# A mixture-of-experts stage as one block, with each tile's results added to the tokens' rows in DRAM

## The reference

```
logits = xf @ router_w + router_b                      # 8 experts
topk_vals, topk_idx = lax.top_k(logits, 2)
gates  = softmax over the two chosen, 0 elsewhere
routed = silu(xf @ w1[e]) * (xf @ w3[e]) @ w2[e]        # for each expert e
y      = sum_e gates[:, e] * routed[e], and two shared experts; both halves weighted 0.5
```

## Time and profile before

| | us |
|---|---|
| median of three runs | 3865.52 (3856.92 to 3866.49) |
| the profiled execution's own time | 3864.73 |
| its span | 3862.7 |

### The profile page before, as it was taken

The page is one execution under the profiler, slowest core; times in us unless marked ns, Lnnn a source line. Parts: engine busy times, 40 slices in busy tenths (PEclk is TensorE's granted clock), DMA queues, the critical chain, the costliest instruction groups (busy, mean ns, idle before and its releaser), DMA issues. The chain is left out here.

```text
span 3862.7 us, 72003 instructions
## 1 busy us (share of the span) xinstructions
PE 3120.2 (81%) x24192; PEld 2382.7 (62%) x24192; DVE 2530.4 (66%) x5327; ACT 1824.5 (47%) x3241; POOL 1631.9 (42%) x1347
## 2 busy tenths in 40 slices
PE   5999688888799889688507999999999996995880
PEld 4888577777688778576404555555555554884660
DVE  5666577877566678555375777777777765774552
ACT  2444244444355445255303666666666664543550
POOL 1665222222366545456552333333333332553665
PEclk9999899999899989799857999999999997987995
DMA  3000000000000022355443324324233221224547
GB/s 110 0 0 0 16 0 0 0 0 0 1 0 0 19 77 74 105 161 158 149 143 101 93 70 114 82 78 111 74 88 100 74 66 64 77 74 156 158 151 281
DMA packets 204552, 292.07 MB, mean 76 GB/s; under 512 B 21472, under 2 KB 136560, under 8 KB 204416
## 3 DMA queue, kind: packets, MB, share of 16 engines
q1 hardware_dynamic: 149760, 189.51, 17.8%
q0 software_dynamic: 27264, 75.01, 5.1%
q10 hardware_dynamic: 27392, 25.83, 2.0%
HBM read 146.47 MB, written 143.28 MB: 75 GB/s over the span
## 5 line engine op out<-in xcount | busy, mean ns | idle before, releaser
L1945 DVE TENSOR_REDUCE neg_max_sb<-s_ps 128x1 f32<-128x512 f32 x1024 | 692.4, 687 | 292.4 <-PE s_ps L1672 271.6
L1835 ACT ACTIVATE prob_sb<-s_ps 128x512 f32<-128x512 f32 x1024 | 602.5, 600 | 393.6 <-PE s_ps L1684 384.3
L1592 POOL TENSOR_TENSOR prob_sb<-prob_sb,band_sb 128x520 f32<-128x520 f32 (+1 forms) x256 | 285.2, 1114 | 715.5 <-ACT prob_sb L1835 715.3
L529 POOL TENSOR_TENSOR f_sq_lo_sb<-f_sq_sb,f_sq_hi_sb 128x512 fp32r<-128x512 f32 x256 | 329.5, 1295 | 348.4 <-ACT f_sq_hi_sb L504 348.4
L1684 PE MATMUL s_ps<-q_stack_sb,k_stack_sb 128*128 128x512 f32 x1024 | 450.9, 441 | 8.0 <-ACT prob_sb L1835 7.5
L1672 PE MATMUL s_ps<-k_stack_sb,q_stack_sb 96*128 96x512 f32 x1024 | 425.9, 419 | 33.6 <-DMA k_stack_sb<-qk_scratch 23.3
L1280 POOL DMA_INDIRECT ranked_rows<-m_y_gated_sb,slot_dest_sb x312 | 328.0, 1051 | 263.5 <-ACT m_y_gated_sb L1261 177.5
L946 POOL DMA_INDIRECT expert_rows<-rows_sb,row_index_sb x256 | 258.0, 1008 | 245.3 <-DVE row_index_sb L1045 173.6
L1684 PEld LDWEIGHTS s_ps<-q_stack_sb,k_stack_sb 128*128 128x128 f32 x1024 | 193.2, 189 | 256.7 <-ACT prob_sb L1835 131.3
L499 ACT ACTIVATE f_relu_sb<-ffn_hp_ps 128x512 f32<-128x512 f32 x256 | 153.4, 599 | 314.6 <-PE ffn_hp_ps L452 314.0
L1705 PE MATMUL pv_ps<-prob_sb,v_ones_sb 128*32 128x512 f32 x2048 | 273.2, 606 | 0.9 <-POOL prob_sb L1592 0.9
(11 more groups left out here) (346 smaller groups left out, 7936.9 us busy)
## 6 DMA issues: line engine op xcount, KB each, us to landing
expert_in_sb<-expert_rows SPq DMA_DIRECT2D x78, 520.0 KB
qk_scratch<-qk_hi_sb SPq DMA_DIRECT2D x128, 256.0 KB
q_stack_sb<-qk_scratch SPq DMA_DIRECT2D x128, 192.0 KB, 4.0
k_stack_sb<-qk_scratch SPq DMA_DIRECT2D x128, 192.0 KB, 4.2
token_results_sb<-ranked_rows SPq DMA_DIRECT2D x32, 512.0 KB, 6.3
token_results_sb<-ranked_rows ACTq DMA_DIRECT2D x32, 512.0 KB, 6.0
qk_scratch<-qk_lo_sb SPq DMA_DIRECT2D x64, 256.0 KB
expert_rows<-zero_rows_sb ACTq DMA_DIRECT2D x16, 520.0 KB, 5.6
```

The costliest lines, as they stand in the source:

```text
L529: nc.gpsimd.tensor_tensor(sql[:, j, :], sq[:, j % 2, :], as_f32(sqh[:, j, :]), ALU.subtract).then_inc(low_ready, 1)
L1592: nc.gpsimd.tensor_tensor(pr, pr, bcast(band[:, off:off + hi - lo].unsqueeze(1), [P, GH, hi - lo]), ALU.mult).then_inc(band_done, 1)
L1835: nc.scalar.activation(prob[:, kt % 2, i, :], s2p[i % 2][:, :], ACT.Exp).then_inc(exp_done, 1)
L1945: nc.vector.tensor_reduce(nm[:, g % 2, 2 * (i % 2) + i // 2, qt:qt + 1], s1p[n % 2][:, :], AXIS_X, ALU.max, negate=True).then_inc(max_done, 1)
```

## The change

It consists of five parts.

1. **GLA.** ACT takes over `norm.normalise` and `o_norm`, as `activation(Identity, bias=-mean*rstd, scale=rstd)`; DVE only makes the factors. SP writes zeros over all of `expert_rows` (70144 rows of 1040 bytes) in four DMAs beside the stage, which ends only when they have landed.
2. **MoE weights.** `prepare` handles the router and the shared experts alone. The routed experts' weights come in 12 pieces inside the dispatch loop: ACT loads and casts one a batch, GpSimd makes the low part.
3. **One block.** Dispatch, table and tiles are one block. The shared experts of batch b-1 run beside the router of batch b. ACT normalises, GpSimd copies the row of the second choice. Only the 4 payload columns behind an expert's last row are zeroed, not whole rows.
4. **Results.** SP stores each batch's `x` (with the shared experts' part) to `token_sums` in DRAM. Each tile's four indirect DMAs have `compute_op=ALU.add` and go to the token's own row there. GpSimd waits, before tile i's four, until those of tile i-1 have landed (`back`), since a token's two rows may stand in tiles that follow each other.
5. **Combine** becomes `result_phase`: eight loads of the sums into `x` with statistics (moe0), or eight copies from DRAM to DRAM into `out` (moe1).

The core of the diff:

```
+                    for b in range(B):
+                        sp.wait_ge(y_added, b + 1)
+                        sp.dma_start(sums[:, b * TILES:(b + 1) * TILES, :],
+                                     core.x[:, b * TILES:(b + 1) * TILES, :]).then_inc(x_stored, 16)
...
+                    for i in range(NT):
+                        pool.wait_ge(ys_ready, i + 1)
+                        pool.wait_ge(dst_ready, i + 1)
+
+                        if i:
+                            pool.wait_ge(back, PER_BACK * i)
+                        else:
+                            pool.wait_ge(x_stored, 16 * B)
+                        for t in range(TILES):
+                            nc.gpsimd.indirect_dma_start(
+                                scratch.sums, bass.IndirectOffsetOnAxis(ap=dst[:, i % META, t:t + 1], axis=0),
+                                ys[:, i % 2, t, :], None, compute_op=ALU.add).then_inc(back, 16)
...
+                    def scale(i):
...
+                        if i >= 2:
+                            act.wait_ge(back, PER_BACK * (i - 1))
...
+                    second(0)
+                    for b in range(B):
+                        if b < len(routed):
+                            weight_low(b)
+                        if b + 1 < B:
+                            second(b + 1)
...
+        def move(engine, i):
+            engine.dma_start(dst[:, i * n:(i + 1) * n, :], src[:, i * n:(i + 1) * n, :]).then_inc(done[i], 16)
...
+                    part = slice(left * i // CLEAR, left * (i + 1) // CLEAR)
+                    sp.dma_start(cleared[:, part, :], bcast(zeros[:, :].unsqueeze(1), [P, part.stop - part.start, TILES * ROW])
+                                 ).then_inc(clear_done[i], 16)
...
+                def o_norm(b):
+                    act.wait_ge(o_off, b + 1)
+                    for t in range(NC):
+                        op = nc.scalar.activation(og[:, t, :], og[:, t, :], ACT.Identity, bias=off[:, t:t + 1],
+                                                  scale=ors[:, t:t + 1])
+                    op.then_inc(on_ready, 1)
```

More of the change, by code:

```diff
@@ L1072, in table_phase @@
-def table_phase(core, name, tables, kept, tab, tail):
-    nc, s = core.nc, core.sem
-    own, limit, tile_no = tables
-    seen, earlier = kept
-    B = core.batches
-    T = B * TOKENS
-    REGION, NT = dispatch_sizes(T)
-    LIM = T // TOKENS
-    with ExitStack() as ctx:
-        ps = core.psum(name + "_ps", [P, EXPERTS], ctx)
-        n = core.sbuf("count", [P, EXPERTS], F32, ctx)
+        zero = core.sbuf("zero_payload", [P, TILES, ROW - DM], F32, ctx)
+        arena = core.sbuf("rows", [P, RB * TOP_K * TILES * ROW], F32, ctx)
@@ L1341, in combine_phase @@
-def combine_phase(core, name, scratch, ctx, out):
+        expert_of, first_row, row_of = (core.sbuf(n, [P, NT], F32, ctx) for n in ("expert_of", "first_row", "row_of"))
+        wt = core.sbuf("tile_weights", [P, 2, 4, KT, P], F32R, ctx)
+        values = core.sbuf("routed_values", [P, 2, 2 * DM], F32, ctx)
+        past, past_tiles = (values[:, i, 0:NT * EXPERTS].rearrange("p (n e) -> p n e", e=EXPERTS) for i in range(2))
+        gate = core.sbuf("slot_gate", [P, META, TILES], F32, ctx)
+        spare = core.sbuf("slot_spare", [P, META, TILES], F32, ctx)
@@ L1342, in combine_phase, with result_phase @@
+        result_phase(core, name + "_c", scratch, out)
+def result_phase(core, name, scratch, out):
     nc, s = core.nc, core.sem
@@ L1363, in store @@
-            def store(b):
-                sp.wait_ge(x_done, b + 1)
-                tiles = slice(b * TILES, (b + 1) * TILES)
-                sp.dma_start(rows[:, tiles, :], core.x[:, tiles, :]).then_inc(stored, 16)
-            for b in range(B):
-                load(sp, b, 0)
-                if out is not None and b >= 2:
-                    store(b - 2)
+            for i in range(0, PARTS, 2):
+                move(sp, i)
             if out is not None:
-                store(B - 2)
-                store(B - 1)
-                sp.wait_ge(stored, 16 * B)
+                for i in range(PARTS):
+                    sp.wait_ge(done[i], 16)
@@ L1377, in _ @@
         @block.scalar
         def _(act):
-            for b in range(B):
-                load(act, b, 1)
-        @block.gpsimd
-        def _(pool):
-            for b in range(B):
-                pool.wait_ge(loaded[b % RING], 32 * (b // RING + 1))
-                nc.gpsimd.tensor_tensor(yb[:, b % RING, 0, :, :], yb[:, b % RING, 0, :, :], yb[:, b % RING, 1, :, :],
-                                        ALU.add).then_inc(summed, 1)
+            for i in range(1, PARTS, 2):
+                move(act, i)
@@ L2122, in gla_stage @@
         turns, st_step = s(name + "_turns"), s(name + "_st_step")
+        CLEAR = 4
+        zeros = core.sbuf("g_zeros", [P, TILES * ROW], F32, ctx)
+        clear_done = [s(f"{name}_cleared{i}") for i in range(CLEAR)]
+        left = scratch.rows.shape[0] // (P * TILES)
+        assert scratch.rows.shape[0] % (P * TILES) == 0
+        cleared = scratch.rows.rearrange("(p n t) d -> p n (t d)", p=P, t=TILES)
         masks_in, zeroed = s(name + "_masks"), s(name + "_zeroed")
```

1165 lines of the change are left out of this document (582 added, 583 removed).

## The result

The changed kernel takes 4208.7 us (median of 4 runs, 4206.2 to 4224.1) where the kernel before takes 3861.2 (4 runs): 1.0913 of it, 95% interval 1.0875 to 1.095. It is slower, as forecast, but by three times the amount: +347 us where +105 were forecast, and above the range's end of 4140. The profiled execution's span is 4208.1 us, against 3862.7.

The account below looks back on a forecast made before the run. No one engine was taken to bound the kernel; each stage has its own limit. MoE without adds -119 us, with GLA -149, the adds +254: 3864.73 + 105 = 3970 us, range 3800 to 4140.

## What to carry over

Before an adding indirect DMA replaces plain writes and a later sum, count its issues: here each took 1.56 us of GpSimd and not 0.97, with rows of 1024 bytes and of 512 alike, and behind a wait for the tile before every one of them is on the path. When a loop is re-ordered across batches, don't add up work per engine: take each buffer that two steps share and read what now stands between its last reader and its next writer, on the reader's engine. And where TensorE pauses in every round, count the lower clock behind it too: here it cost 2.7 us a batch beside 3.2 of standing.
